# Attention scores computed in 64-row tiles, as two accumulation steps on the same rows, in planes for pairs of heads

## The reference, cut to what matters

```python
z  = layernorm(x)                       # 4 x 1024 x 256
zn = layernorm(z) * ln_scale + ln_bias
qkv = (zn @ w_qkv).reshape(b, n, 16, 16, 3)      # 16 heads of 16 features
scores = einsum('bhqd,bhkd->bhqk', q, k) / 4
att = softmax(scores)
z  = z + (att @ v) @ w_proj + b_proj
x  = x + layernorm(z)
x  = x + layernorm(ffn(layernorm(x)))   # a gated layer, and 8 experts for 512 chosen tokens
```

## Time and profile before

| | |
|---|---|
| median of 3 runs | 1066.33 us (1063.77 to 1066.88) |
| the profiled execution | 1063.63 us |
| its span, first to last instruction | 1061.8 us |
| mean granted clock of TensorE | 0.967 |

### The profile page before, as it was taken

How to read it: one execution, slowest core, us unless ns; L and a number is a source line. 1 busy time by engine, 2 the same in 40 slices (tenths; PEclk the granted TensorE clock), 3 DMA queues, 4 the chain that set the end, 5 groups by cost and what they waited for, 6 DMA issues and landing times.

```text
span 1061.8 us, 14474 instructions
## 1 busy us (share of the span) xinstructions
PE 974.1 (92%) x5348; PEld 384.1 (36%) x5348; DVE 868.5 (82%) x1763; ACT 601.0 (57%) x700; POOL 251.3 (24%) x303
## 2 busy tenths in 40 slices
PE   4379999999999999999999999999999999947994
PEld 3122332323344334333352343332422433236763
DVE  5288888899888989998879889979899899164766
ACT  3025677677765775767757766677666656811110
POOL 4060001101623121246304312154042020612103
PEclk9597999999999999999999999999999999987997
DMA  9805100510250203200611032014310000240001
GB/s 175 134 1 68 54 18 24 73 48 1 57 94 12 80 1 52 66 13 32 109 51 41 2 45 68 9 41 88 73 41 1 1 1 2 80 158 21 1 1 59
DMA packets 46534, 50.27 MB, mean 47 GB/s; under 512 B 8432, under 2 KB 39424, under 8 KB 46080
## 3 DMA queue, kind: packets, MB, share of 16 engines
q1 hardware_dynamic: 45120, 47.51, 21.1%
q10 hardware_dynamic: 960, 0.79, 0.6%
q0 software_dynamic: 384, 1.05, 0.3%
HBM read 13.94 MB, written 8.91 MB: 22 GB/s over the span
## 4 chain that ended last, share of the span: by engine, by line
PE 72%; DVE 20%; DMA 2%; ACT 2%; issue 1%; POOL 1%; SPq 1%; ACTq 0%; DVEq 0%; POOLq 0%
PE sc L846 20%; PE obank L860 16%; DVE mx L1069 14%; PE ring L832 13%; PE ring L747 9%; PE ring L769 4%; PE sc L936 4%; PE ring L739 2%; DVE st L1011 2%; PE ring L886 2%; ACT prob L672 1%; DVE hid L1033 1%; DMA idx_in<-index_t 1%; DMA kp<-parts 1%; PE ring L880 1%
## 5 line engine op out<-in xcount | busy, mean ns | idle before, releaser
L1069 DVE TENSOR_REDUCE mx<-ring 128x1 f32<-128x512 f32 x1024 | 650.1, 685 | 80.2 <-PE ring L832 72.5
L672 ACT ACTIVATE prob<-sc 128x1024 f32<-128x1024 f32 x512 | 501.0, 1022 | 268.4 <-PE sc L846 268.3
L860 PE MATMUL obank<-prob,vaug 128*32 128x512 f32 x2048 | 273.2, 606 | 0.7 <-ACT prob L672 0.7
L846 PE MATMUL sc<-qp,kp 112*128 112x512 bf16 x1024 | 267.7, 383 | 0.9 <-ACT prob L672 0.2
L832 PE MATMUL ring<-kp,qp 48*128 48x512 bf16 x1024 | 224.8, 391 | 30.3 <-issue 16.2
L832 PEld LDWEIGHTS ring<-kp,qp 48*128 48x128 bf16 x1024 | 57.5, 93 | 357.3 <-DVE mx L1069 189.2
L846 PEld LDWEIGHTS sc<-qp,kp 112*128 112x128 bf16 x1024 | 83.8, 98 | 114.7 <-issue 38.9
L505 POOL TENSOR_SCALAR parts<-resid 128x1024 bf16<-128x1024 f32 x14 | 14.7, 1050 | 326.2 <-DVE resid L1059 325.8
L860 PEld LDWEIGHTS obank<-prob,vaug 128*32 128x32 f32 x2048 | 40.3, 108 | 61.8 <-issue 52.4
L747 PE MATMUL ring<-w,yT 128*128 128x256 f32 x192 | 50.0, 403 | 0.7 <-ACT yT L598 0.7
L739 PE MATMUL ring<-ident,zn 128*128 128x128 f32 x128 | 21.1, 300 | 24.9 <-DVE zn L1027 12.8
(11 more groups left out here) (178 smaller groups left out, 789.5 us busy)
## 6 DMA issues: line engine op xcount, KB each, us to landing
kp<-parts SPq DMA_DIRECT2D x96, 128.0 KB, 5.4
qp<-parts SPq DMA_DIRECT2D x180, 64.0 KB, 2.6
x_sb<-x SPq DMA_DIRECT2D x7, 1024.0 KB, 6.0
out<-hid SPq DMA_DIRECT2D x4, 1024.0 KB, 4.6
x_scratch<-x SPq DMA_DIRECT2D x3, 1024.0 KB, 4.4
kp<-ew SPq DMA_DIRECT2D x1, 2048.0 KB, 8.4
x_sb<-x SPq DMA_DIRECT2D x2, 512.0 KB, 4.6
qp<-mp SPq DMA_DIRECT2D x64, 4.0 KB, 1.7
```

What stands on the lines that cost most here:

```text
L672: nc.scalar.activation(prob[:, e % 2, 2 * a:2 * a + 2, :].rearrange("p g n -> p (g n)"), sbuf2[a][:, :], ACT.Exp, scale=0.25).then_inc(s_f ...
L846: ins = nc.tensor.matmul(dst[:, j * HALF:(j + 1) * HALF], kp[0:KM, h, kt * P:(kt + 1) * P], qp[0:KM, qh, h, :], start=True, stop=True)
L860: ins = nc.tensor.matmul(obank[i * VW:(i + 1) * VW, :], vaug[:, b % 2, kt, c0:c0 + VW], prob[:, v % 2, i, :], start=(kt == 0), stop=(kt == ...
L1069: nc.vector.tensor_reduce(mx[:, u % 2, n:n + 1], src[:, :], AX.X, ALU.max).then_inc(rv_free, 1)
```

## The change

`KM` becomes 50: the score product of a head is now two products that are accumulated in the same bank. Both lie on rows 0 to 49 for the first head of a pair and on rows 64 to 113 for the second. The index of `kp` and `qp` behind the partition is now a plane: `plane_of` gives, for a head, the plane with the three largest terms (0) and the one with the other three (1), eight heads at a time, so that heads 0, 2, 4, 6 and 1, 3, 5, 7 of a group share planes on different rows. Ones (keys) and maxima (queries) stand on two rows of plane 1 only. The stacking DMAs write four neighbouring planes in place of every second head. The fixed rows are filled by four DMAs of 2 rows x 4 planes for the keys, none for the queries. The maxima of a unit go with four DMAs in place of two, as its heads lie on both halves; the columns of the maxima are ordered to match. The order within a slot stays.

```diff
-KM = 64 + KR
+KM = KR + 2
-STACK = [(par, (64 * (par ^ (r // 3)) + r % 3 * HD), k, q) ...
+STACK = [(par, r // 3 * 4, 64 * par + r % 3 * HD, k, q) ...
...
 def max_column(t, j):
     h, qt, kh = max_item(t, j)
-    return (h * QT + qt) * 2 + kh
+    return ((h % 2 * 2 + h // 2) * QT + qt) * 2 + kh
+
+def plane_of(h, plane):
+    return h // 8 * 8 + 4 * plane + h % 8 // 2
...
-        fixed = resid[0:16, :].bitcast(bf16)
+        fixed = resid[0:2, 0:HALF].bitcast(bf16)
...
-                        sp.dma_start(kp[rows, h0:h0 + 7:2, :], parts[src, 0, k, :]).then_inc(s_pack[0], 16)
+                        sp.dma_start(kp[rows, h0:h0 + 4, :], parts[src, 0, k, :]).then_inc(s_pack[0], 16)
...
-            sp.dma_start(kp[48:64, :, :], fixed[:, 0:N] ... .to_broadcast([16, H, N])).then_inc(s_fixed, 16)
-            sp.dma_start(qp[48:64, :, :, :] ... fixed[:, N:N + HALF] ... .to_broadcast([16, NH * H, HALF])).then_inc(s_fixed, 16)
+            for par in range(2):
+                for h in (0, 8):
+                    first = plane_of(h, 1)
+                    sp.dma_start(kp[64 * par + KR:64 * par + KM, first:first + 4, :],
+                                 fixed[:, :] ... .to_broadcast([2, 4, N])).then_inc(s_fixed, 16)
...
-                    for j in range(2):
-                        sp.dma_start(qp[KR + j:KR + j + 1, qh, g * GH:(g + 1) * GH, :],
-                                     mp[:, u % 2, j, :]).then_inc(s_mrow[u % 2], 16)
+                    first = plane_of(g * GH, 1)
+                    for par in range(2):
+                        for j in range(2):
+                            row = 64 * par + KR + j
+                            sp.dma_start(qp[row:row + 1, qh, first:first + 2, :],
+                                         mp[GH // 2 * QT * par:GH // 2 * QT * (par + 1), u % 2, j, :])\
+                              .then_inc(s_mrow[u % 2], 16)
...
-                    for j in range(2):
-                        h = g * GH + 2 * a + j
-                        ins = nc.tensor.matmul(dst[:, j * HALF:(j + 1) * HALF], kp[0:KM, h, kt * P:(kt + 1) * P],
-                                               qp[0:KM, qh, h, :], start=True, stop=True)
+                    for plane in range(2):
+                        h = plane_of(g * GH + 2 * a, plane)
+                        for j in range(2):
+                            rows = slice(64 * j, 64 * j + (KM if plane else KR))
+                            ins = nc.tensor.matmul(dst[:, j * HALF:(j + 1) * HALF], kp[rows, h, kt * P:(kt + 1) * P],
+                                                   qp[rows, qh, h, :], start=plane == 0, stop=plane == 1)
...
-            nc.vector.memset(fixed[:, 0:N], 1.0)
-            nc.vector.memset(fixed[:, N:2 * N], 0.0).then_inc(s_src, 1)
+            nc.vector.memset(fixed[:, :], 1.0).then_inc(s_src, 1)
```

More of the change, by code:

```diff
@@ L28 @@
 PRODUCTS = [(0, 0), (1, 0), (0, 1), (2, 0), (1, 1), (0, 2)]
-STACK = [(par, (64 * (par ^ (r // 3)) + r % 3 * HD), k, q) for r, (k, q) in enumerate(PRODUCTS) for par in range(2)]
+STACK = [(par, r // 3 * 4, 64 * par + r % 3 * HD, k, q) for r, (k, q) in enumerate(PRODUCTS) for par in range(2)]
 ONES = struct.unpack("<f", struct.pack("<HH", 0x3F80, 0x3F80))[0]
@@ L335, in pack_step @@
                             sp.wait_ge(s_av, SL * (b - 1) + (SL // 2 if c < 2 else SL))
-                    par, row, k, q = STACK[n if n < len(STACK) else (n - len(STACK)) // NH]
-                    rows, h0, src = slice(row, row + HD), c // 2 * 8 + par, slice(par * 64, par * 64 + 64)
+                    par, plane, row, k, q = STACK[n if n < len(STACK) else (n - len(STACK)) // NH]
+                    rows, h0, src = slice(row, row + HD), c // 2 * 8 + plane, slice(par * 64, par * 64 + 64)
                     if n < len(STACK):
-                        sp.dma_start(kp[rows, h0:h0 + 7:2, :], parts[src, 0, k, :]).then_inc(s_pack[0], 16)
+                        sp.dma_start(kp[rows, h0:h0 + 4, :], parts[src, 0, k, :]).then_inc(s_pack[0], 16)
                     else:
                         qh = n % NH
-                        sp.dma_start(qp[rows, qh, h0:h0 + 7:2, :],
+                        sp.dma_start(qp[rows, qh, h0:h0 + 4, :],
                                      parts[src, 1, q, qh * HALF:(qh + 1) * HALF]).then_inc(s_pack[1], 16)
@@ L349, in _ @@
             sp.wait_ge(s_src, 1)
[L350 to L354, removed]
+            for par in range(2):
+                for h in (0, 8):
+                    first = plane_of(h, 1)
+                    sp.dma_start(kp[64 * par + KR:64 * par + KM, first:first + 4, :],
+                                 fixed[:, :].rearrange("p (o n) -> p o n", o=1).to_broadcast([2, 4, N]))                      .then_inc(s_fixed, 16)
             sp.dma_start(idx_in[:, 0, :], index_b.rearrange("(p c) -> p c", p=P)).then_inc(s_idxin, 16)
@@ L365, in _ @@
                     sp.wait_ge(s_third, 1)
-                for par, row, k, q in STACK:
+                for par, plane, row, k, q in STACK:
                     if k == part:
-                        sp.dma_start(kp[row:row + HD, par:par + 7:2, :], parts[par * 64:par * 64 + 64, 0, k, :])\
+                        sp.dma_start(kp[row:row + HD, plane:plane + 4, :], parts[par * 64:par * 64 + 64, 0, k, :])\
                           .then_inc(s_pack[0], 16)
             sp.wait_ge(s_third, 2)
-            for par, row, k, q in STACK:
-                sp.dma_start(qp[row:row + HD, 1, par:par + 7:2, :], parts[par * 64:par * 64 + 64, 1, q, HALF:N])\
+            for par, plane, row, k, q in STACK:
+                sp.dma_start(qp[row:row + HD, 1, plane:plane + 4, :], parts[par * 64:par * 64 + 64, 1, q, HALF:N])\
                   .then_inc(s_pack[1], 16)
-            sp.wait_ge(s_fixed, 32)
+            sp.wait_ge(s_fixed, 64)
             sp.wait_ge(s_norm["z"], 1)
@@ L657, in _ @@
                     sc.wait_ge(s_third, 2)
-                for par, row, k, q in STACK:
+                for par, plane, row, k, q in STACK:
                     if q == part:
-                        nc.scalar.dma_start(qp[row:row + HD, 0, par:par + 7:2, :],
+                        nc.scalar.dma_start(qp[row:row + HD, 0, plane:plane + 4, :],
                                             parts[par * 64:par * 64 + 64, 1, q, 0:HALF]).then_inc(s_q0, 16)
@@ L829, in max_products @@
                         h, qt, kh = max_item(t, j)
-                        rows, h = slice(64 * (h % 2), 64 * (h % 2) + KR), g * GH + h
+                        rows, h = slice(64 * (h % 2), 64 * (h % 2) + KR), plane_of(g * GH + h, 0)
                         dst = open_r("max", t, j)
@@ L1138, in _ @@
             nc.vector.tensor_copy(iota[:, :], iotai[:, :]).then_inc(s_idx, 1)
-            ve.wait_ge(s_fixed, 32)
+            ve.wait_ge(s_fixed, 64)
             for c in range(2):
```

4 lines of the change are left out of this document (2 added, 2 removed).

## The result

The changed kernel takes 1073.58 us (median; 1072.89 to 1075.34), the kernel before 1066.56. The ratio is 1.0072, with an interval of 1.0059 to 1.0085. The forecast was 1060.5 and the range ended at 1069.5; the profiled execution has a span of 1073.5 us against 1061.8.

What follows compares the result with a forecast made beforehand. TensorE was taken to end a plain slot, only 0.2 us above VectorE. Steady part -6.0, maxima rows +1.1 and start -0.9 sum to -5.8, from 1066.3 to 1060.5 us; range 1052 to 1069.5.

Steps and rivals of the forecast that it cites:

- (1): TensorE scores: eight products run as pairs, a slot's scores in 0.87 us, with 0 for the second product's weight load.
- (2): TensorE changes of tile: plain slots lose two of four, fill slots net 0, some transpose-fill places pay; 3.0 us given back.
- (3): Plain slots: step falls from 2.61 to 2.49 us, 9.0 us gained; steady part -6.0 after 3.0 given back.
- the 75 that gain 0.12: Plain slots over all images, chosen as following no transpose and outside VectorE's limits, that make the 9.0 us gain.
- (4): Maxima rows on SP: four DMAs per unit in place of two leave little slack for the scores; +1.1 us, bounds 0 and +6.
- upper bound of 6: Largest cost reckoned for late maxima rows: +6 us if each of ten units comes 0.5 us late.
- a rival, at 1065.4: Maxima rows late: they cost +6 us rather than +1.1; chance 0.10.
- (5): Start, up to the first max product: smaller fixed-row filling makes stacking start and land earlier; -0.9 us in sum.
- the -0.4: Start: with 64 KB of filling in four DMAs, SP waits for data, so the first stacking DMA is issued 0.4 us earlier.
- (6): Smaller memset, permuted maxima columns and the last twelve slots, where ScalarE paces: no effect, 0.
- The rival with exposed loads: Scores: each head's second product waits 0.10 us for weights on four pairs a slot, 1138; chance 0.08, shared with serial pairs.

Runs made afterwards that it cites:

- e1: Changed kernel with the maxima of a unit sent by two DMAs, each writing both halves; 1068.40 us, ratio 1.0030 to the kernel before.
- e11: Kernel before with the fill moved behind the value products and ScalarE reading it behind both exponentials; 1091.66 us, ratio 1.0246.
- e12: e1's kernel with the fill items of neighbouring slots put into one slot (54 pairs); 1092.37 us, ratio 1.0250 to the kernel before.
- e13: Kernel before with the fill items of neighbouring slots put into one slot; 1095.74 us, ratio 1.0289.
- e3: Changed kernel with the fill moved behind the first pair of max products; 1097.87 us, ratio 1.0307 to the kernel before.
- e5: e1's kernel with the fill moved behind the value products; 1116.05 us, ratio 1.0476 to the kernel before.
- e8: Changed kernel run again unaltered; 1074.43 us, ratio 1.0083 to the kernel before.
- e7: Kernel before with each of the two DMAs of a unit's maxima cut in two, nothing else; 1069.79 us, ratio 1.0040.
- e14: e1's kernel with the two large fixed transfers of the kernel before; 1067.82 us, ratio 1.0018 to the kernel before.
- e15: e12's kernel with the two large fixed transfers of the kernel before; 1092.25 us, ratio 1.0247 to the kernel before.

## Why the prediction was wrong, step by step

**(1) Scores as pairs, 0.87, no exposed load between the two products of a head: right.** The second product of a head starts 0.22 behind the first in 1012 of 1024 cases. The Trainium skill (TensorE: Matmul & The Clock Gate, Part 3, "The mechanism") says that a weight load overlaps a running matmul only when row groups differ, though the same section also lets a load into the background weight buffer go ahead. The trace does not agree with the first of these for bf16 loads behind products on the same rows. The prediction had priced that rival at 0.10 a pair, 1138 in all.

**(2) Changes of tile: the count was right, "a slot with a fill item ... 0" was wrong.** This is the step that failed. It counted scores-to-fill as 0.10, the price read between bf16 products. Behind a change of tile a f32 128-row fill pays that and its first weight load, which was hidden under the 112-row scores: 0.11 in the 72 slots with projections or feed-forward products, 0.06 in the 42 with transposes of 128 columns. In e1 all fill together is 9.6 us longer than in the kernel before, and the sum had nothing for it. A row of before could have told it: at 482.42 the fill's loads begin while the last score product streams, cover that the change takes away. e11 shows the load exposed in the old layout, e12 and e13 that it is paid once per visit.

**(3) The plain slot, 2.49: right, and the sum by kinds of slot was not.** e1 less before, neither of which waits for maxima, from first score to first score:

| slots | number | us |
|---|---|---|
| plain, not behind a transpose | 55 | -5.2 |
| plain, behind a transpose | 31 | -5.8 |
| with a transpose, no fill | 44 | +7.6 |
| with fill, no transpose | 98 | +1.9 |
| with fill and a transpose | 16 | +5.2 |

Together +3.7 where -6.0 was forecast, 9.7 more; the missing loads (9.6) are as large as the difference. That the two agree so well is in part luck, for the places differ. The slots with fill took +7.1, and the prediction had 3.0 for them; the longer fill replaces waits for ring banks that stood there before. The slots without fill gained 3.3 rather than 9.0. Plain slots among plain ones gained the 0.12 forecast where VectorE had no other work, those behind a transpose 0.19 where 0 was forecast. Slots with a transpose lose 0.10 or more: most of them were counted among the 75 that gain 0.12, but the change from transpose to scores (0.10) falls into them, and where the extra reduction comes first, their first pair of maxima takes 0.52, as VectorE is behind. VectorE's slack in a plain slot is now 2.49 less 2.40, 0.09, and was 0.21.

**(4) Maxima rows, +1.1: right mechanism, wrong size.** The fourth row was reckoned to land 3 x 0.59 + 1.7 = 3.5 after the subtraction; it takes 3 x 0.71 + 1.8 = 3.9, for 3.6 of cover. The issue time of a DMA of 4 KB was taken for one of 2 KB, and the smaller DMA is the slower one. Measured by e1: 4.2 to 5.2 us, near the upper bound of 6. It was also a rival, at 1065.4.

**(5) The start, -0.9: not borne out.** One part came: in profiles whose projections all take 0.59, SP's first stacking DMA is issued at 19.9 to 20.2 us with small fixed rows (e3, e5, e8) and at 20.8 to 20.9 with large ones (e7, e11, e13), as the -0.4 had it. But the stacking behind it takes longer, not shorter, so that the first max product is 1.5 later on average (45.1 against 43.6). The prediction took the fixed rows for a load on the queue that stacking would be rid of. In the medians of e14 and e15 at most 0.6 of it shows. Contiguous runs do nothing.

**(6) The rest, 0:** the last eleven slots differ by 0.2 in e1.

The sum of what was measured: +3.7 in the slots and +4.2 for the maxima are 7.9, against 7.0 in the medians; with 1.5 for the start they are 9.4, against 11.7 in the spans. The two ways of counting differ by 4.7, because the profiled execution of before lies 2.9 below its median (1066.56) and the one after 1.8 above.

The rival with exposed loads had the right phenomenon in the wrong place (between scores, priced at 71 us, rather than at the fill). No run beat the kernel before; the nearest, e14, is 1.9 us (0.2%) slower.

## What to carry to other kernels

When a product's tile changes, ask what was loaded under it: the next group's first weights lose their cover too, and that is read from where the loads stand, not from the gap between two products of the cheap kind. A move in one engine's order must be checked on the others that share its slot: here the fill spaced the max products, set when ScalarE reads, and covered VectorE's side work. A transfer cut in two is two transfers of another form; take its issue time from a row with that form, or leave the term its upper bound.

## What the runs showed of the hardware

A change between 128-row and 64-row tiles costs 0.10 us each way (0.96 for 0.87, 0.32 for 0.23). The first f32 128-row weight load behind a change of tile lies open, which costs another 0.11 with products of 256 or 512 columns and 0.06 with 128; behind the value products, 128 rows by 32 columns, it lies open as well (e11). Two bf16 products after each other on the same 64 rows cost nothing extra (0.22 from one to the next). A DMA of 2 KB into one partition takes SP 0.62 to 0.72 us to issue, one of the same bytes into two partitions 0.50, and one of 4 KB into one partition 0.58 (medians 0.63, 0.50 and 0.58). With 64 KB rather than 1 MB of fixed rows in front, the same stacking (12 transfers of 128 KB and 24 of 64 KB) took longer to the first max product in every profile, 24.3 to 24.6 against 20.5 to 24.0 us; nothing here says why.
